# Row halves for two heads at once: maxima and scores of a transformer layer on one core of Trainium2

## The chip, the core and the metric

The kernel runs on one core of a Trainium2 chip. The core has five engines with a queue each: TensorE (PE in the profile; PEld are its weight loads), VectorE (DVE), ScalarE (ACT), GpSimd (POOL) and SyncE (SP), which here issues nearly all transfers. Operands lie in SBUF, products land in eight banks of PSUM, 512 f32 columns wide. The metric is the time of one execution in microseconds (us).

## The reference

Four sequences of 1,024 rows and 256 columns go through a residual block without softmax and then through a block with 16 query heads, 4 key/value heads of 16 channels, and 8 experts of which each row takes 2.

```
x = x + attn_linear(layernorm(x))
h = rmsnorm(layernorm(x)); q, k, v = split(h @ wqkv.T); q, k = rope(q), rope(k)
scores = einsum("bqhd,bkhd->bhqk", q, k) * 16**-0.5
scores = where(causal, scores, min)
attn = softmax(scores) @ v
x = x + attn @ wo.T; h = rmsnorm(x)
out = x + sum over the two best experts of weight * ((silu(h @ w1.T) * (h @ w3.T)) @ w2.T)
```

The change is in the line with scores and in the softmax of the line after next.

## The kernel before

**Tiling.** A head group is one key head with its four query heads (GRP); there are 16 (4 sequences, 4 key heads). The 1,024 query rows are two chunks of 512 (CH; r is 0 or 1), keys go in tiles of 128 (kt). Chunk 0 needs key tiles 0 to 3, chunk 1 all eight. On the diagonal the widths are 512, 384, 256 and 128.

**Exact products in bf16.** q and k are f32, split into three bf16 parts each (stage `split`). Six of the nine products of parts count; a head has 16 channels, so the six make one contraction of 96 rows. `split_store` writes the parts to DRAM (`parts`, 3 x 320 rows), and `stack` reads them back into a *stack*, an SBUF buffer with 96 rows of queries for four heads and 96 of keys. Keys' rows and queries' rows need another order, so the three `KPARTS` are loaded apart, with two transfers each. There are three stacks (NSTACK), so loads run ahead of use.

**Maxima** (`max`, L1871 to L1890 on TensorE, L1699 to L1708 on VectorE). For each query tile of 128 rows (jj) and head, TensorE forms all products with the keys up to the diagonal and adds a mask of -1e38 by a product of `identb` and `causal` (L1889, or L1879 for four heads at once). VectorE reduces the columns to one maximum per row (`mx`). In chunk 1 a unit is one head: 512 columns against chunk 0's keys (L1883) in one bank, w own columns (L1888) and the mask in the next, one reduce over CH + w columns. `maxT` (L1894) transposes the maxima, VectorE negates them into two bf16 parts (`mneg_parts`, L1715 and L1717), and SyncE writes these to rows 96 and 97 of the stack (L979).

**Scores** (`score`, L1901). A contraction of 98 rows now gives score minus maximum, 512 columns (or less on the diagonal) of one head per bank; up to four narrow ones share a bank. ScalarE takes the exponential into `probs` (L1254), GpSimd masks the diagonal tiles (L1115), and `pv` (L1915) forms the weighted sums of the four heads in four column groups of the array, 17 columns each, in f32.

**Order.** `plan()` walks through all steps once, before the kernel is built, with a table of assumed durations and due times, and picks for each engine the next step; all five instruction orders and the PSUM banks (RING, seven of them; the eighth holds the weighted sums) come from it. `seat` gives a step its banks. Where `keep_warm` sees TensorE idle it puts in a `warm` step (L1804, or L1801 where two neighbouring banks are free: 64-row products in either half of the array). Each engine runs its list in order. The experts' steps are due last and fill gaps from the third sequence on.

## Time and profile before

| | |
|---|---|
| median of 3 runs | 1,112.95 us (1,111.84 to 1,113.57) |
| the profiled execution | 1,115.85 us, span 1,114.1 us |
| granted TensorE clock, mean | 0.996 of full speed |
| busy: PE, DVE, ACT, POOL | 1,078.1, 737.3, 576.5, 408.4 us |
| maxima's reduces on VectorE | 352, 346.8 us |
| exponentials of the scores on ScalarE | 608, 309.0 us |

The span is the stretch from the first to the last instruction of the profiled execution; its own time is 1.75 us longer. PE's busy time counts each matmul to its end, though the next one starts earlier, so the distance of starts is what one costs. What the rows say of a wait is in the engine's idle time before a group and in the releaser that ended it.

### The profile page before, as it was taken

The numbers are of one execution on the slowest core, as the hardware profiler recorded it, in microseconds if no ns is written. First come the engines' busy times: TensorE is split into PE (matmuls) and PEld (weight loads), VectorE is DVE, ScalarE is ACT, GpSimd is POOL, SyncE is SP. The second block draws the span as 40 slices with busy tenths as digits, with TensorE's granted clock in tenths as the row PEclk, the third lists the DMA queues.
The fourth block names the chain that finished last, engine by engine and source line by source line (L and its number), as shares of the span: only waits on it lengthen the run. The fifth ranks groups of instructions, "written<-read, shape, count | busy, mean of one in ns | idle before, by whom it ended". The sixth has DMA issues, their size and how long they took to land.

```text
span 1114.1 us, 20589 instructions
## 1 busy us (share of the span) xinstructions
PE 1078.1 (97%) x7168; PEld 677.9 (61%) x7168; DVE 737.3 (66%) x1522; ACT 576.5 (52%) x1108; POOL 408.4 (37%) x476
## 2 busy tenths in 40 slices
PE   6999999999999999999999999999999999999997
PEld 5666543554544333444344454446667999999996
DVE  4697998677677977578967669624347555555552
ACT  3554477556658887756556765562332222233220
POOL 1020413616541154321244522445544753333332
PEclk9999999999999999999999999999999999999999
DMA  6324222232226466551253441124342543222221
GB/s 178 121 84 136 69 73 62 79 102 73 86 90 177 137 206 189 160 147 44 53 138 89 110 115 41 35 61 94 83 103 54 106 86 49 46 45 44 45 44 11
DMA packets 85717, 102.07 MB, mean 92 GB/s; under 512 B 17104, under 2 KB 73296, under 8 KB 85616
## 3 DMA queue, kind: packets, MB, share of 16 engines
q1 hardware_dynamic: 71312, 81.13, 25.5%
q0 software_dynamic: 14304, 19.63, 9.5%
q8 instruction: 59, 0.97, 0.4%
q14 instruction: 42, 0.34, 0.1%
HBM read 55.89 MB, written 41.01 MB: 87 GB/s over the span
## 4 chain that ended last, share of the span: by engine, by line
PE 75%; DVE 16%; issue 2%; DMA 2%; ACT 2%; SPq 1%; POOL 1%; DVEq 0%; POOLq 0%
PE psum L1970 15%; PE psum L1986 11%; PE psum L1915 9%; DVE mx L1708 8%; PE psum L1962 8%; PE psum L1901 8%; PE psum L1888 4%; PE psum L1883 4%; PE psum L1869 3%; PE psum L1922 3%; PE psum L1823 2%; PE psum L1889 1%; PE psum L1950 1%; PE psum L1845 1%; PE psum L1937 1%
## 5 line engine op out<-in xcount | busy, mean ns | idle before, releaser
L1708 DVE TENSOR_REDUCE mx<-psum 128x1 f32<-128x640 f32 (+6 forms) x352 | 346.8, 1022 | 73.5 <-PE psum L1889 68.9
L1254 ACT ACTIVATE probs_mem<-psum 128x512 f32<-128x512 f32 (+1 forms) x608 | 309.0, 586 | 142.1 <-PE psum L1901 140.5
L1115 POOL TENSOR_SCALAR_AFFINE_SELECT probs_mem<-probs_mem 128x512 f32<-128x512 f32 x128 | 82.1, 642 | 293.0 <-ACT probs_mem L1254 292.5
L1160 POOL DMA_INDIRECT out<-yout,labels x71 | 112.7, 1588 | 207.9 <-DVE yout L1774 151.8
L1901 PE MATMUL psum<-stack_mem 98*128 98x512 bf16 (+3 forms) x768 | 172.5, 327 | 4.2 <-DVE mx L1708 3.5
L1915 PE MATMUL psum<-probs_mem,v 128*17 128x512 f32 (+3 forms) x1536 | 160.4, 492 | 1.6 <-POOL probs_mem L1115 1.3
L1888 PE MATMUL psum<-stack_mem 96*128 96x256 bf16 (+3 forms) x448 | 124.8, 311 | 0.8 <-DVE mx L1708 0.6
L1901 PEld LDWEIGHTS psum<-stack_mem 98*128 98x128 bf16 x768 | 63.9, 98 | 86.3 <-DVE mx L1708 31.1
L1883 PE MATMUL psum<-stack_mem 96*128 96x512 bf16 x256 | 97.2, 385 | 5.9 <-DVE mx L1708 3.2
L1962 PE MATMUL psum<-w_mem,blockT 128*128 x200 | 96.8, 607 | 1.9 <-issue 1.8
L1889 PE MATMUL psum<-causal,identb 128*128 128x128 bf16 x448 | 96.2, 220 | 0.0
L1986 PE MATMUL psum<-w_mem,gatedT 128*128 x384 | 91.3, 381 | 0.0
L1970 PE MATMUL psum<-blockT,probs_mem 128*128 128x128 f32 x736 | 89.6, 275 | 0.0
L1970 PE MATMUL psum<-blockT,stack_mem 128*128 128x128 f32 x736 | 89.5, 275 | 0.0
L1970 PEld LDWEIGHTS psum<-blockT,probs_mem 128*128 128x128 f32 x736 | 87.6, 192 | 1.2
L1970 PEld LDWEIGHTS psum<-blockT,stack_mem 128*128 128x128 f32 x736 | 87.5, 192 | 1.2
L1282 ACT ACTIVATE gated<-psum 128x512 f32<-128x512 f32 x48 | 28.7, 598 | 108.2 <-PE psum L1962 58.3
L1986 PEld LDWEIGHTS psum<-w_mem,gatedT 128*128 128x128 f32 x384 | 70.5, 190 | 14.4 <-issue 6.4
L1145 POOL DMA_INDIRECT routed<-hrow,route_mem x64 | 64.4, 1006 | 35.8 <-issue 18.1
L1758 DVE COPY blockT<-psum 128x256 f32<-128x256 f32 x71 | 30.0, 422 | 70.6 <-PE psum L1950 70.5
L1888 PEld LDWEIGHTS psum<-stack_mem 96*128 96x128 bf16 x448 | 44.0, 98 | 32.0 <-issue 12.6
L1889 PEld LDWEIGHTS psum<-causal,identb 128*128 128x128 bf16 x448 | 43.6, 97 | 32.1 <-issue 0.6
(209 smaller groups left out, 1518.9 us busy)
## 6 DMA issues: line engine op xcount, KB each, us to landing
block<-routed SPq DMA_DIRECT2D x71, 129.0 KB, 2.1
w_mem<-in_w13T SPq DMA_DIRECT2D x16, 512.0 KB, 5.1
qk_parts<-w_mem SPq DMA_DIRECT2D x16, 384.0 KB, 2.5
stack_mem<-qk_parts SPq DMA_DIRECT2D x32, 192.0 KB, 3.2
...
```

The costliest lines, as they stand in the source:

```text
L1115: e.affine_select(pb[:, :, q0:q0 + P], pb[:, :, q0:q0 + P], [[0, GRP], [1, P]], ALU.is_ge, 0.0, base=0, channel_multiplier=-1).then_inc(se ...
L1160: e.indirect_dma_start(out_rows, bass.IndirectOffsetOnAxis(ap=labels[w % NLABEL].bitcast(I32)[:, 0:1], axis=0), youts[w % NYOUT], None, bo ...
L1254: e.activation(probs[m % 2][:, hh:hh + n, q0:CH], grid(turn[step][0][:, 0:n * (CH - q0)], n), ACT.Exp, scale=float(HD) ** -0.5).then_inc(s ...
L1708: e.tensor_reduce(to, took, AX.X, ALU.max).then_inc(sem["max"], 1)
L1883: e.matmul(bk[:, 0:CH], rows_of, s[0:STACK, 0, GRP, :], start=True, stop=True)
L1888: e.matmul(to, rows_of, s[0:STACK, r, GRP, 0:w], start=True, stop=False)
L1889: m = e.matmul(to[:, w - P:w], identb, causal, start=False, stop=True)
L1901: m = e.matmul(bk[:, i * (CH - q0):(i + 1) * (CH - q0)], s[0:STACK + NMAX, kt // TPR, GRP, kt % TPR * P:(kt % TPR + 1) * P], s[0:STACK + N ...
L1915: m = e.matmul(pv_bank[32 * hh:32 * hh + HD + 1, q0:CH], v1[:, b, kt, g, :], pb[:, hh, q0:CH], start=(kt == KEYS[r][0]), stop=(kt == KEYS[ ...
L1962: m = e.matmul(bk, blockT[w % 2][:, k], w13_s[:, k, bass.ds(offset[w] + half * FFN, FFN)], start=(k == 0), stop=(k == KD - 1))
L1970: m = e.matmul(bk[:, c * P:(c + 1) * P], slots[w % NSLOT][:, k, half * FFN + c * P:half * FFN + (c + 1) * P], blockT[w % 2][:, k], start=( ...
L1986: m = e.matmul(bk[:, 0:D], rowsT[:, k * P:(k + 1) * P], w2_mem[:, bass.ds(offset[w] + k * D, D)], start=(k == 0), stop=(k == KF - 1))
```

## The change

- **Halves.** The array is used as two halves of 64 rows (SIDES). Heads 0 and 1 of a group lie on rows 0 to 63, heads 2 and 3 on rows 64 to 127 (PER_SIDE). Each matmul of `max` and `score` has 64 rows or fewer and comes twice, once for each half, into neighbouring banks.
- **Maxima** are formed from four of the six products of parts, the 64 rows of the first stack (FIRST). The mask is added in pieces that fit 64 rows: 64 columns with `causal`'s triangle, then 128 columns. In chunk 1 the products against chunk 0's keys are units of their own, with their own column of `mx`, and a `tensor_tensor` joins both sets. Reduces take both halves at once.
- **Scores** are two passes per half: 64 rows of the first stack, then 34 of the second (two products and the two rows of negated maxima). A step covers both halves in two banks; ScalarE's exponential takes up to 1,024 columns.
- **Stacks.** Two in place of one: three buffers of the first (NFIRST), two of the second (NSECOND). Outside, in DRAM, `q_image` and `k_image` hold the rows in the stacks' order, parts repeated as needed (96 rows per head in place of 48), so each split unit is stored by three transfers (SPLIT_STORES) and a stack is loaded by 3 (first) or 4 (second, mostly for both chunks at once). The negated maxima go by four transfers.
- **Order.** `plan()` gets the new units, two banks for each score, and a preference to stay in one division of the array (STAY; `division`: row halves, column groups, or neither). `warm` has only its f32 form.

```diff
-KPARTS = (3, 2, 1)
-STACK = sum(KPARTS) * HD
+SIDES = 2
+PER_SIDE = GRP // SIDES
+SIDE = P // SIDES
+FIRST, SECOND = 4 * HD, 2 * HD
 NMAX = 2
+SPLIT_STORES = 3
...
-NSTACK = 3
+NFIRST, NSECOND = 3, 2
...
+STACK_LOADS = (SIDES + 1, 2 * SIDES)
...
-    if r:
-        return [(jj, hh, 1, CH, (jj + 1) * P) for jj in range(TPR) for hh in range(GRP)]
-    units = []
+    units = [(False, jj, h0, 1, CH) for jj in range(TPR) for h0 in range(PER_SIDE)] if r else []
     for jj in range(TPR):
-        w = (jj + 1) * P
-        nh = GRP if jj < 2 else 2
-        units += [(jj, h0, nh, w if jj < 2 else CH, w) for h0 in range(0, GRP, nh)]
+        n = PER_SIDE if jj < 2 else 1
+        units += [(True, jj, h0, n, (jj + 1) * P) for h0 in range(0, PER_SIDE, n)]
     return units
-def max_banks(r, u):
-    return 1 if not r and max_units(r)[u][0] == 0 else 2
 def heads_in(r, kt):
-    n = min(GRP, CH // (CH - max(kt * P - r * CH, 0)))
-    return n, range(0, GRP, n)
+    n = min(PER_SIDE, CH // (CH - max(kt * P - r * CH, 0)))
+    return n, range(0, PER_SIDE, n)
...
+        own, jj, h0, n, w = max_units(r)[u]
+        joined = 0.25 * (r > 0 and u == len(max_units(r)) - 1)
+        return ("PE", n * (w + 3 * SIDE * own) / 2400 + 0.02), ("DVE", 0.07 + SIDES * n * w / 960 + joined)
...
         if stage == "score":
             n = heads_in(r, kt)[0]
-            return ("PE", n * w / 2400 + 0.01), ("ACT", 0.06 + n * w / 1200)
+            return ("PE", 2 * n * w / 2400 + 0.02), ("ACT", 0.06 + SIDES * n * w / 1200)
         last = kt == KEYS[r][-1]
-        return (("PE", 0.23 + w / 600), ("ACT", 0.49)) if last else (("PE", 0.23 + w / 600),)
+        return (("PE", 0.13 + w / 600), ("ACT", 0.49)) if last else (("PE", 0.13 + w / 600),)
...
+    def division(step):
+        return {"score": 1, "max": 1, "pv": 2}.get(step[0], 0)
...
-            return [("max", *at, len(max_units(at[2])) - 1)] + [("maxT", *chunk_at(m))] * (m >= 0)
+            freed = [s for n in group_back(b, at[1], NSECOND) for s in last_scores(*n)]
+            return [("max", *at, len(max_units(at[2])) - 1)] + [("maxT", *chunk_at(m))] * (m >= 0) + freed
...
-            return [("maxT", *at[:3])] + [pvs[m]] * (m >= 0)
+            return [("maxT", *at[:3])] + [("stack", b, at[1], c, 1) for c in (range(at[2] + 1) if not at[1] else [QR - 1])] + [pvs[m]] * (m >= 0)
...
-        n = max_banks(*step[3:]) if step[0] == "max" else KD if step[:2] == ("gram", 0) else 1
+        n = SIDES if step[0] in ("max", "score") else KD if step[:2] == ("gram", 0) else 1
...
+            later = STAY * (engine == "PE" and division(step) != divided)
+            key = (0, due + later, start) if start <= free + 0.05 else (1, start, due)
...
-            end += COLD * (start > clock[engine] + COLD)
+            end += COLD * (start > clock[engine] + COLD or division(step) != divided)
...
-                    r0, n = ((NH * HD, 2 * HK), (0, P), (P, P))[u]
-                    q.wait_ge(*slot("split_store", 4, m - 4))
...
+                    q.wait_ge(*slot("split_store", 4, m - 4, SPLIT_STORES))
...
-                    e.dma_start(parts[b][:, c, r0:r0 + n, :].rearrange("s r t -> r s t"), splits[m % 2][0:n]).then_inc(sem[f"split_store{m % 4}"], 16)
+                    for part, at_rows in enumerate(found):
...
+                        e.dma_start(to, splits[m % 2][0:n, part].unsqueeze(1).broadcast_to([n, len(at_rows), CH])).then_inc(sem[f"split_store{m % 4}"], 16)
                 elif stage == "stack":
...
-                    e.dma_start(s[to:to + nk * HD, c, GRP, :], parts[b][0:nk, c, NH * HD + g:QK:NKV, :].rearrange("s i t -> i s t")).then_inc(landing, 16)
-                    e.dma_start(s[to:to + nk * HD, c, 0:GRP, :].rearrange("p h t -> p (h t)"),
-                                q_rows(b, qp, c)[g].unsqueeze(1).broadcast_to([HD, nk, GRP * CH])).then_inc(landing, 16)
+                    b, g, c, of_second = at
+                    n = b * NKV + g
+                    landed(q, "split_store", 4, 3 * (QR * b + c + 1), SPLIT_STORES)
+                    if not of_second:
+                        s, landing = first[n % NFIRST], sem[f"first{n % NFIRST}_{c}"]
+                        if n >= NFIRST:
+                            first_read(q, *HEAD_GROUPS[n - NFIRST])
+                        e.dma_start(s[:, c, PER_SIDE, :], key_rows(b, g)[c, SECOND:].unsqueeze(0).broadcast_to([SIDES, FIRST, CH])).then_inc(landing, 16)
+                        for side in range(SIDES):
+                            e.dma_start(s[side * SIDE:(side + 1) * SIDE, c, 0:PER_SIDE, :].rearrange("p h t -> p (h t)"), side_rows(b, g, side)[c, SECOND:]
+                                        ).then_inc(landing, 16)
+                    else:
+                        s, landing = second[n % NSECOND], sem[f"second{n % NSECOND}_{c}"]
+                        if n >= NSECOND:
+                            second_read(q, *HEAD_GROUPS[n - NSECOND])
+                        cs = slice(0 if g else c, c + 1)
+                        for side in range(SIDES):
+                            to = s[side * SIDE:side * SIDE + SECOND, cs]
+                            e.dma_start(to[:, :, PER_SIDE, :], key_rows(b, g)[cs, 0:SECOND].rearrange("c r t -> r c t")).then_inc(landing, 16)
+                            e.dma_start(to[:, :, 0:PER_SIDE, :].rearrange("p c h t -> p c (h t)"), side_rows(b, g, side)[cs, 0:SECOND].rearrange("c r t -> r c t")).then_inc(landing, 16)
                 elif stage == "maxT":
                     b, g, r = at
...
+                    if n >= NSECOND:
+                        second_read(q, *HEAD_GROUPS[n - NSECOND])
+                    for side in range(SIDES):
+                        for c in range(NMAX):
+                            row, of = side * SIDE + SECOND + c, side * PER_SIDE * TPR
+                            e.dma_start(second[n % NSECOND][row:row + 1, r, 0:PER_SIDE, :].rearrange("p h t -> p (h t)"), mneg_parts[of:of + PER_SIDE * TPR, c, :]
+                                        ).then_inc(sem[f"max_load{m % 2}"], 16)
...
+                    scored = grid(turn[step][0], SIDES)[:, :, 0:n * (CH - q0)].rearrange("p s (h q) -> p s h q", h=n)
                     q.wait_ge("score_mm", nth[step])
                     q.wait_ge("pv_mm", m - 1)
-                    e.activation(probs[m % 2][:, hh:hh + n, q0:CH], grid(turn[step][0][:, 0:n * (CH - q0)], n), ACT.Exp, scale=float(HD) ** -0.5).then_inc(sem["exp"], 1)
+                    e.activation(probs[m % 2].rearrange("p (s h) q -> p s h q", s=SIDES)[:, :, hh:hh + n, q0:CH], scored, ACT.Exp, scale=float(HD) ** -0.5).then_inc(sem["exp"], 1)
...
+                    own, jj, h0, n, w = max_units(r)[u]
+                    to = mx[:, r if own else 2].rearrange("p (s h j) -> p s h j", s=SIDES, h=PER_SIDE)[:, :, h0:h0 + n, jj]
+                    took = grid(turn[step][0], SIDES)[:, :, 0:n * w].rearrange("p s (h k) -> p s h k", h=n)
                     q.wait_ge("max_mm", nth[step])
                     q.wait_ge("maxT_mm", chunk(b, g, r) - 1)
                     e.tensor_reduce(to, took, AX.X, ALU.max).then_inc(sem["max"], 1)
+                    if r and u == len(max_units(r)) - 1:
+                        q.wait_ge("max", nth[step])
+                        e.tensor_tensor(mx[:, 1], mx[:, 1], mx[:, 2], ALU.max).then_inc(sem["join"], 1)
...
-                    jj, h0, nh, pitch, w = max_units(r)[u]
-                    s = stack[(b * NKV + g) % NSTACK]
-                    buffer_loaded(q, b, g, r)
-                    q.wait_ge("const", 4)
-                    if w == P and not r:
-                        e.matmul(grid(bk, GRP), identb, causal.unsqueeze(1).broadcast_to([P, GRP, P]), start=True, stop=False)
-                    for c in range(nh):
-                        rows_of = s[0:STACK, r, h0 + c, jj * P:(jj + 1) * P]
-                        if r:
-                            e.matmul(bk[:, 0:CH], rows_of, s[0:STACK, 0, GRP, :], start=True, stop=True)
-                        to = bk[:, CH:CH + w] if r else bk[:, c * pitch:c * pitch + w]
-                        if w == P and not r:
-                            m = e.matmul(to, rows_of, s[0:STACK, r, GRP, 0:w], start=False, stop=c == nh - 1)
-                        else:
-                            e.matmul(to, rows_of, s[0:STACK, r, GRP, 0:w], start=True, stop=False)
-                            m = e.matmul(to[:, w - P:w], identb, causal, start=False, stop=True)
+                    own, jj, h0, n, w = max_units(r)[u]
+                    s = first[(b * NKV + g) % NFIRST]
+                    first_loaded(q, b, g, r)
+                    q.wait_ge("const", 6)
+                    for c in range(n):
+                        halves = [(slice(i * SIDE, (i + 1) * SIDE), bk[:, i * CH + c * w:i * CH + (c + 1) * w]) for i in range(SIDES)]
+                        for half, to in halves:
+                            m = e.matmul(to, s[half, r, h0 + c, jj * P:(jj + 1) * P], s[half, r if own else 0, PER_SIDE, 0:w], start=True, stop=not own)
+                        if own:
+                            for half, to in halves:
+                                e.matmul(to[:, w - SIDE:w], diagonal[half, 0:P], causal[half, 0:SIDE], start=False, stop=False)
+                            for half, to in halves:
+                                m = e.matmul(to[:, w - P:w], diagonal[half, SIDE:], causal[half], start=False, stop=True)
                     m.then_inc(sem["max_mm"], 1)
                 elif stage == "maxT":
                     b, g, r = at
-                    q.wait_ge("max", nth["max", b, g, r, len(max_units(r)) - 1])
+                    if r:
+                        q.wait_ge("join", b * NKV + g + 1)
+                    else:
+                        q.wait_ge("max", nth["max", b, g, r, len(max_units(r)) - 1])
                     e.transpose(bk[0:16, 0:P], mx[:, r], ident).then_inc(sem["maxT_mm"], 1)
                 elif stage == "score":
                     b, g, r, kt, hh = at
-                    q0, n, s = max(kt * P - r * CH, 0), heads_in(r, kt)[0], stack[(b * NKV + g) % NSTACK]
-                    q.wait_ge(*slot("max_load", 2, chunk(b, g, r), NMAX))
-                    q.wait_ge("set", 6)
+                    q0, n, m_of = max(kt * P - r * CH, 0), heads_in(r, kt)[0], b * NKV + g
+                    w, tile = CH - q0, slice(kt % TPR * P, (kt % TPR + 1) * P)
+                    q.wait_ge(*slot("max_load", 2, chunk(b, g, r), NMAX * SIDES))
+                    q.wait_ge("set", 7)
+                    first_loaded(q, b, g, r)
+                    second_loaded(q, b, g, r)
                     for i in range(n):
-                        m = e.matmul(bk[:, i * (CH - q0):(i + 1) * (CH - q0)], s[0:STACK + NMAX, kt // TPR, GRP, kt % TPR * P:(kt % TPR + 1) * P],
-                                     s[0:STACK + NMAX, r, hh + i, q0:CH], start=True, stop=True)
+                        for s, rows_in in ((first[m_of % NFIRST], FIRST), (second[m_of % NSECOND], SECOND + NMAX)):
+                            for side in range(SIDES):
+                                half = slice(side * SIDE, side * SIDE + rows_in)
+                                m = e.matmul(bk[:, side * CH + i * w:side * CH + (i + 1) * w], s[half, kt // TPR, PER_SIDE, tile], s[half, r, hh + i, q0:CH],
+                                             start=rows_in == FIRST, stop=rows_in != FIRST)
```

**TensorE, batch 1, second head group, chunk 1.** In the first fence each head's maxima are three multiplies (L1883 against chunk 0's keys, L1888 own keys, L1889 mask), and L1901 are scores, L1915 weighted sums, L1922 the output product.

```order
L1883 MATMUL psum<-stack_mem 128x512
L1888 MATMUL psum<-stack_mem 128x256
L1889 MATMUL psum<-causal,identb 128x128
L1901 MATMUL psum<-stack_mem 128x512
L1883 MATMUL psum<-stack_mem 128x512
L1888 MATMUL psum<-stack_mem 128x256
L1889 MATMUL psum<-causal,identb 128x128
L1915 MATMUL psum<-probs_mem,v 17x512 x4
L1883 MATMUL psum<-stack_mem 128x512
L1888 MATMUL psum<-stack_mem 128x256
L1889 MATMUL psum<-causal,identb 128x128
L1901 MATMUL psum<-stack_mem 128x384 x4
```

The same group and chunk after, at two places of the changed order (L1952 products, L1956 and L1958 mask pieces, L1980 scores, L1994 weighted sums, L1875 a warm-up): the products against chunk 0's keys first,

```order
L1952 MATMUL psum<-stack_mem 128x512 x4
L1980 MATMUL psum<-stack_mem 128x512 x4
L1994 MATMUL psum<-probs_mem,v 17x128 x4
L1980 MATMUL psum<-stack_mem 128x512 x4
L1952 MATMUL psum<-stack_mem 128x512 x4
L1875 MATMUL psum<-ident 128x128
L1980 MATMUL psum<-stack_mem 128x512 x8
L1994 MATMUL psum<-probs_mem,v 17x512 x4
```

and those against its own keys behind them.

```order
L1952 MATMUL psum<-stack_mem 128x256 x2
L1956 MATMUL psum<-causal,diagonal 128x64 x2
L1958 MATMUL psum<-causal,diagonal 128x128 x2
L1980 MATMUL psum<-stack_mem 128x256 x8
L1994 MATMUL psum<-probs_mem,v 17x512 x4
L1952 MATMUL psum<-stack_mem 128x384 x2
L1956 MATMUL psum<-causal,diagonal 128x64 x2
L1958 MATMUL psum<-causal,diagonal 128x128 x2
```

Three multiplies per head became six per pair of heads on own keys and one per head against chunk 0's; scores are twice as many multiplies, each of half the rows. Between scores, sums and f32 work the array's division now changes each time.

**SyncE at the start: stores and first loads of sequence 0, chunk 0.** Before (L962 stores of split parts, L970 keys and L971 queries of a stack):

```order
L962 DMA qk_parts<-w_mem 64x3x512
L962 DMA qk_parts<-w_mem 128x3x512 x2
L970 DMA stack_mem<-qk_parts 48x1x512
L971 DMA stack_mem<-qk_parts 48x1x2048
L970 DMA stack_mem<-qk_parts 32x1x512
L971 DMA stack_mem<-qk_parts 32x1x2048
L970 DMA stack_mem<-qk_parts 16x512
L971 DMA stack_mem<-qk_parts 16x2048
```

After (L1015 stores of the images, L1024 and L1026 the first stack, L1035 and L1036 the second):

```order
L1015 DMA q_image<-w_mem 128x3x512
L1015 DMA q_image<-w_mem 128x2x512
L1015 DMA q_image<-w_mem 128x512
L1024 DMA stack_mem<-k_image 128x1x512
L1026 DMA stack_mem<-q_image 64x1024 x2
L1035 DMA stack_mem<-k_image 32x512
L1036 DMA stack_mem<-q_image 32x1024
L1035 DMA stack_mem<-k_image 32x512
L1036 DMA stack_mem<-q_image 32x1024
```

Three stores became nine (the last three stand here), and the six loads ahead of the first maximum became three, with four more behind them for the scores.

## Rows read from the trace of the kernel before

**Rows 1.** The page, part 1: busy time, share of the span, instructions of each engine.
```profile
PE 1078.1 (97%) x7168; PEld 677.9 (61%) x7168; DVE 737.3 (66%) x1522; ACT 576.5 (52%) x1108; POOL 408.4 (37%) x476
```
**Rows 2.** Groups of TensorE by form, then its timeline (start us, us, engine line).
```profile
L1901 PE MATMUL psum<-stack_mem 98*128 98x512 bf16 x384 | 110.0, 380 | 3.2 <-DVE mx L1708 2.8 <-ACT probs_mem L1254 0.2
...
309.68 1.04 PE L1901 MATMUL psum<-stack_mem 98*128 98x512 bf16 x4
...
310.81 0.22 PE L1888 MATMUL psum<-stack_mem 96*128 96x128 bf16 x1
310.87 0.22 PE L1889 MATMUL psum<-causal,identb 128*128 128x128 bf16 x1
```
**Rows 3.** The page, part 4: the chain that ended last, by engine.
```profile
PE 75%; DVE 16%; issue 2%; DMA 2%; ACT 2%; SPq 1%; POOL 1%; DVEq 0%; POOLq 0%
```
**Rows 4.** Who waited for whom: us in total, times, longest.
```profile
ACT probs_mem L1254 <- PE psum L1901: 140.5, 141, 4.6
...
DVE mx L1708 <- PE psum L1889: 68.9, 77, 4.0
...
PEld psum L1901 <- DVE mx L1708: 31.1, 51, 2.3
...
PEld psum L1883 <- DVE mx L1708: 21.3, 41, 1.0
```
**Rows 5.** Warm-ups in row halves: their group by form, then TensorE's timeline at two places.
```profile
L1801 PE MATMUL psum<-causal,identb 64*128 64x256 bf16 x56 | 4.4, 272 | 0.1
...
36.02 0.49 PE L1801 MATMUL psum<-causal,identb 64*128 64x256 bf16 x6
...
305.83 0.72 PE L1804 MATMUL psum<-ident 128*128 128x128 f32 x5
306.49 0.39 PE L1801 MATMUL psum<-causal,identb 64*128 64x256 bf16 x4
```
**Rows 6.** TensorE's timeline from a score through column groups to a maximum.
```profile
299.98 0.33 PE L1901 MATMUL psum<-stack_mem 98*128 98x384 bf16 x1
300.24 1.05 PE L1915 MATMUL psum<-probs_mem,v 128*17 128x512 f32 x8
301.22 0.28 PE L1888 MATMUL psum<-stack_mem 96*128 96x256 bf16 x1
```
**Rows 7.** Weighted sums of 128 columns: by form, and one step in the timeline.
```profile
L1915 PE MATMUL psum<-probs_mem,v 128*17 128x128 f32 x256 | 13.2, 278 | 0.1
...
745.21 0.41 PE L1915 MATMUL psum<-probs_mem,v 128*17 128x128 f32 x8
```
**Rows 8.** The maxima's reduces on VectorE, by form.
```profile
L1708 DVE TENSOR_REDUCE mx<-psum 128x1 f32<-128x1024 f32 x64 | 75.9, 1218 | 16.9 <-PE psum L1889 16.7
...
L1708 DVE TENSOR_REDUCE mx<-psum 128x1 f32<-128x640 f32 x64 | 50.1, 810 | 13.8 <-PE psum L1889 13.5
```
**Rows 9.** Exponentials of 512 columns on ScalarE, by form.
```profile
L1254 ACT ACTIVATE probs_mem<-psum 128x512 f32<-128x512 f32 x480 | 255.6, 608 | 117.5 <-PE psum L1901 116.1 <-issue 0.5
```
**Rows 10.** SyncE's and TensorE's timeline: stack loads, negated maxima, a chunk's first score.
```profile
63.28 0.62 SPq L970 DMA_DIRECT2D stack_mem<-qk_parts  x1
...
371.46 1.16 SPq L979 DMA_DIRECT2D stack_mem<-mneg_parts  x2
...
380.74 0.39 PE L1901 MATMUL psum<-stack_mem 98*128 98x512 bf16 x1
...
90.84 1.19 PE L1901 MATMUL psum<-stack_mem 98*128 98x512 bf16 x5
```
**Rows 11.** Windows of 50 us: PE, PEld, DVE, ACT, POOL busy (count), clock, DMA share, GB/s.
```profile
100.00:150.00 50.00, 49.12 (x324) 26.83 (x324) 47.33 (x88) 21.32 (x40) 14.40 (x15) 1.00 0.23 72
...
250.00:300.00 50.00, 49.24 (x331) 23.92 (x330) 33.98 (x49) 31.98 (x64) 26.91 (x27) 1.00 0.27 79
...
350.00:400.00 50.00, 47.84 (x361) 18.85 (x363) 46.77 (x93) 40.35 (x74) 11.82 (x16) 1.00 0.59 170
...
500.00:550.00 50.00, 47.39 (x333) 21.91 (x332) 44.08 (x97) 30.29 (x61) 10.88 (x15) 0.98 0.22 60
```

158 lines of the change are left out of this document (86 added, 72 removed), and 1 row of the table WORK_OF.

## The prediction

> **What bounds the kernel now.** Page first: TensorE is busy 97% of the span, VectorE 66% [rows 1]. A busy TensorE isn't a full one: 512-column multiplies that last 380 ns start 0.22 us apart ((1.04 - 0.38) / 3), 128-column ones 0.06 us apart [rows 2]. I multiplied these distances by the order's counts: a column costs 0.42 ns in bf16, four times that in f32 and twice in an f32 transpose. The maxima then take 150 us, scores 123, weighted sums 123 (four heads together in column groups), experts 389, all else 170: some 955 us of 1,114, and the rest is switches, short starts and waits. The chain of waits agrees: 75% TensorE, 16% VectorE [rows 3]. The table of waits says what the rest is. TensorE's loads wait for the maxima's reduces to give banks back (31.1 and 21.3 us), and the reduces wait for their products (68.9 us); ScalarE waits 140.5 us for scores [rows 4]. So TensorE is the bound and VectorE the next one; ScalarE and GpSimd have room.
>
> **1. Columns saved in the maxima.** Now, per head group: chunk 0 streams 7,168 columns (5,120 of products, 2,048 of mask), chunk 1 15,360 (8,192 against chunk 0's keys, 5,120, 2,048). After, each matmul has 64 rows and a half of the array. If two halves run together, a pair costs one: chunk 0 has 2 x (1,280 + 4 x 192) = 4,096, chunk 1 8 x 512 + 4,096 = 8,192. Saved: 10,240 columns x 16 groups = 163,840, or 320 x 0.217 us = **-69 us**. That halves do run together is in the trace: three pairs of 64-row, 256-column warm-ups took 0.49 us where one multiply takes 0.27, so 0.11 us per pair, the time of one [rows 5].
>
> **2. Scores.** 98 rows become 64 + 34 on either half: four multiplies for two heads where there were two. Two passes on two halves stream what two full passes did: **0**, if rows 5 hold for accumulating pairs too.
>
> **3. Switches of the array's division.** After a 384-column score at 299.98 the sums in column groups start at 300.24, where 300.14 was due; after their two passes of 0.43 us the next maximum starts at 301.22, where 301.11 was due [rows 6]. Full to row halves is the same: a 128-column warm-up started at 306.28 (305.83 + 0.72 - 0.27), the halves at 306.49, 0.10 late [rows 5]. So 0.10 us each way. Before, scores and maxima shared the full array with all f32 work; after, they have a division of their own. Counted over the whole order without warm-ups, switches go from 370 to 595: 225 x 0.097 = **+22 us**.
>
> **4. Small multiplies.** The mask becomes a 64- and a 128-column pair per product pair, so six loads and six multiplies stand where w = 128 streams only 0.133 us. The densest rate shown is four loads and four multiplies in a pass of 0.107 us, 0.027 us each [rows 7]: 6 x 0.027 = 0.16, +0.03 us in 64 places, 2 us. If a 64-column pair needed 2 x 0.027 wherever it stands, 256 pairs cost +7 us. With some ns of offset in each pair I take **+3 us**. TensorE's sum: -69 + 22 + 3 = **-44 us**.
>
> **5. VectorE.** A reduce costs 1.06 ns per column ((1,218 - 810) / 384) and about 0.13 us fixed [rows 8]. Columns stay the same; 22 reduces per group become 20 and a join of 128x16. Before 22.5 us, after 22.2 + 0.2: **0**. It is what I expect to be late next.
>
> **6. ScalarE.** 608 exponentials become 320 of up to 1,024 columns. At 608 ns for 512 columns [rows 9], of which 0.43 us stream, that saves at most 0.18 x 288 = 52 us of an engine that waits for TensorE. On the path **0**; without the cover it would help.
>
> **7. SyncE, and what stands behind it.** Its transfers go from 657 to 753, about 0.58 us each [rows 10]. Negated maxima go in four issues in place of two, +1.2 us. Behind them stand stack loads and the packs; who waits is the scores. At the tightest place past the start they land with room: issued at 371.46, first score at 380.74 [rows 10], over 8 us later. Hidden. At the start nothing hides them: the last unit's store of queries is three issues, not one (+1.2), and twice the bytes must land; against that, three loads and not six (0.62 us each) stand ahead of the first maximum (-1.9); then come four issues of negated maxima (+1.2) and the second stack. Bounds 0 and +6, taken **+2 us**. A score now holds two banks of seven; no row prices that, and it is in the range.
>
> **How much arrives.** Of ten stretches of 50 us from 100 to 600, VectorE is busy 95, 94 and 88% in three; the rest lie at 63 to 84%, as 250:300 [rows 11]. In the three a faster TensorE only waits longer for banks, unless the order shifts work. In the other seven, and after 600, where expert blocks fill what attention leaves, it can arrive. I take two thirds: -29 us, with the start -27, and the 1 us that the reduces wait less is **-28 us**. The profiled execution took 1,115.85 us (span 1,114.1), so 1,087.9 by its own time. The median of the runs is 2.9 us under it: **1,085 us**.
>
> A rule of the skill speaks against the change. The Trainium skill, TensorEngine Tiling (Array Packing), section PSUM Bottleneck, says that tiling speeds TensorE but not the emptying of PSUM, which may then bind. By the three full stretches the trace agrees; by the other seven it doesn't yet.
>
> **Rivals.**
> - *VectorE takes over.* For it: the 52 us of loads that wait for reduces [rows 4]; and the whole order is a compromise between the two engines, so that a stretch at 75% may already be held by VectorE's bursts. Then only a third of 44 arrives: -15, and with the start 1,100 us. Against it: 68.9 us in which the reduces themselves wait for products. Chance 0.18.
> - *All of it arrives*, since products come sooner and the reduces' own waits shrink: -44 and up to 4 more, with the start 1,068 us. 0.13.
> - *Rate of small multiplies, mild.* If in row halves a load with its multiply takes the 0.055 us at which full 128-column ones follow each other [rows 2], the products on own keys cost 6 x 0.055 in place of (w + 192) x 0.42 ns, 30 us in all, and 128-column scores 7 us more: TensorE -10, with the start 1,105 us. 0.05.
> - *Slower.* The same mechanism from 0.060 us on: there it costs the 47 us that columns and switches leave. At 0.062 us it is +52 us, so TensorE +5 and 1,120 us. Halves that don't overlap when they accumulate are its end: maxima 164 us in place of 82, scores 246 in place of 123, about 1,270 us. The 0.027 us of rows 7 and the warm-ups of rows 5 speak against it; but rows 7 load 17 columns, not 128, and rows 5 stream 256, so neither shows a 128-column load in 0.027. 0.10.
> - *The change does what it says and nothing arrives*: 1,111 to 1,115. 0.04.
>
> The Trainium skill, TensorE: Matmul & The Clock Gate, section "Wait — 56ns, not 53.3ns?", gives about 62 ns of sequencer time per multiply with hardware decode off, the slow rival's case; the four multiplies of a pass in rows 7 speak against that here.
>
> **How the numbers follow.** Forecast (1,072 to 1,097) 0.50, VectorE 0.18, all 0.13, mild rate 0.05, slower 0.10, nothing 0.04. The likeliest is 1,085. From 1,066 to 1,108 lie the forecast, VectorE, mild rate and half of "all": about 0.8. The three runs lie within 0.16%, so 0.2% is about what can be told. Faster 0.86; within 0.2% 0.04; slower 0.10.
>
> **What would show it.** Steps 1 and 2: in the timeline the two halves' multiplies start together, a pair of 512 columns every 0.22 us; right if the maxima's multiplies per group fit in some 5 us. Step 3: 0.1 us at each change between scores, sums and f32 work. Step 4: a chain of load, 64 and 128 columns of 0.08 us behind its product; 0.17 would be the mild rival. Step 5: reduces still some 345 us in all, TensorE's waits for them longer than 52 us, their waits for products under 69. Step 7: first score at about 93 us, not 91. The prediction is wrong if the halves start one behind the other, or if VectorE stands above 90% through most of 100 to 600.

## The result, and the profile after

The changed kernel takes 1,123.15 us (median of 6 runs, 1,122.41 to 1,127.17); the kernel before, on the same chip, 1,113.26. The ratio is **1.0091, 95% interval 1.0068 to 1.0114**: 10 us slower, where I forecast 28 us faster. The profiled execution took 1,122.6 us (span 1,120.9).

The page of the changed kernel, parts 1, 4 and 5:

```profile
PE 1059.8 (95%) x8560; PEld 651.0 (58%) x8560; DVE 747.9 (67%) x1510; ACT 560.9 (50%) x820; POOL 411.1 (37%) x477
...
PE 66%; DVE 17%; SPq 5%; DMA 4%; ACT 3%; issue 3%; POOL 1%; DVEq 0%; POOLq 0%; ACTq 0%
...
L1782 DVE TENSOR_REDUCE mx<-psum 128x2 f32<-128x1024 f32 (+2 forms) x320 | 344.3, 1111 | 67.7 <-PE psum L1958 42.7
L1324 ACT ACTIVATE probs_mem<-psum 128x1024 f32<-128x1024 f32 (+1 forms) x320 | 289.5, 936 | 141.6 <-PE psum L1980 140.2
```

TensorE is 2 points less busy than in [rows 1] over a longer span. In the chain its share falls from 75 to 66% [rows 3]; VectorE stays, and what has grown is SyncE's queue with the transfers, from 3 to 9%. The work itself went as predicted, which TensorE's timeline shows (start us, us, engine line, tiles, count):

```profile
299.96 0.41 PE L1994 MATMUL psum<-probs_mem,v 128*17 128x128 f32 x8
300.30 0.23 PE L1952 MATMUL psum<-stack_mem 64*128 64x128 bf16 x2
300.37 0.19 PE L1956 MATMUL psum<-causal,diagonal 64*128 64x64 bf16 x2
300.40 0.22 PE L1958 MATMUL psum<-causal,diagonal 64*128 64x128 bf16 x2
300.45 0.22 PE L1952 MATMUL psum<-stack_mem 64*128 64x128 bf16 x2
...
300.60 1.03 PE L1980 MATMUL psum<-stack_mem 64*128 64x512 bf16 x8
301.64 0.28 PE L1952 MATMUL psum<-stack_mem 64*128 64x256 bf16 x2
...
301.83 0.29 PE L1952 MATMUL psum<-stack_mem 64*128 64x256 bf16 x2
...
301.97 0.24 PE L1958 MATMUL psum<-causal,diagonal 64*128 64x128 bf16 x2
302.14 1.05 PE L1994 MATMUL psum<-probs_mem,v 128*17 128x512 f32 x8
303.12 0.34 PE L1952 MATMUL psum<-stack_mem 64*128 64x384 bf16 x2
...
313.03 0.39 PE L1952 MATMUL psum<-stack_mem 64*128 64x512 bf16 x2
```

Two multiplies of 512 columns, one on each half, take 0.39 us together (313.03), what one takes alone (0.38). The eight score multiplies from 300.60 are four pairs, each second pair adding to what the one before it left; with 0.38 us for the last pair they start (1.03 - 0.38) / 3 = 0.22 us apart. Behind a 128-column product (300.30) its masks start 0.07 and 0.10 us later, and the next product 0.15. A product's last mask starts at 301.97 and would let a successor of the same division start at 302.03 (an estimate: 0.06 us for 128 columns, as in [rows 2]); the weighted sums start at 302.14, so the change of division costs 0.1 us.

To see where the time went I added up, over the whole trace, the distances from each multiply's start to the next, and split each into what its columns stream, up to 0.1 us at a change of division, up to 5 ns of issue, and a rest, called stalls below. All of it is worked out from the records of the one profiled execution of each kernel, and good to 1 or 2 us; "maxima" and "scores" are the streamed columns at full clock (us):

| | maxima | scores | changes | warm-ups | issue | stalls | other | all |
|---|---|---|---|---|---|---|---|---|
| before | 150.2 | 122.9 | 37.2 | 9.3 | 20.5 | 70.8 | 687.6 | 1,098.5 |
| after | 84.5 | 125.5 | 61.6 | 19.0 | 16.7 | 111.2 | 687.5 | 1,105.9 |

So 66 us were saved, and the changes of division cost 24, as predicted. **Forty us of stalls** took the rest, more than half of what there was before on top of it, and the warm-ups that the planner puts into such gaps doubled (+9.7). Who waits for whom (us in total, times, longest):

```profile
ACT probs_mem L1324 <- PE psum L1980: 140.2, 126, 10.3
...
DVE mx L1782 <- PE psum L1958: 42.7, 49, 3.6
...
PEld psum L1980 <- DVE mx L1782: 42.4, 69, 1.8
...
PEld psum L1952 <- DVE mx L1782: 34.2, 55, 2.4
...
PEld psum L1952 <- ACT probs_mem L1324: 26.9, 43, 1.9
...
DVE mx L1782 <- PE psum L1952: 23.0, 24, 2.7
```

TensorE's loads now wait 76.6 us for the reduces, where it was 52.4 [rows 4]. The reduces wait for two kinds of product now, 42.7 and 23.0 us. A load's wait is not yet a stall, since loads run ahead of the multiplies. Sorted by what released the late multiply or its load (worked out from the records), the stalls behind the maxima's steps on VectorE grow from 16 to 26 us, **those behind ScalarE's exponentials from 6 to 17**, those behind GpSimd from 3 to 6; 36 before and 44 after show no wait that released them. So it is not VectorE alone that TensorE runs into.

The windows that answer to [rows 11], and two more, show no engine behind TensorE that is full (the number before the last two is the granted clock):

```profile
100.00:150.00 50.00, 44.53 (x362) 25.74 (x360) 41.90 (x83) 16.20 (x23) 13.14 (x13) 0.93 0.38 124
250.00:300.00 50.00, 45.37 (x407) 18.89 (x407) 37.63 (x49) 32.29 (x47) 30.64 (x31) 1.00 0.47 128
350.00:400.00 50.00, 45.92 (x452) 21.80 (x452) 36.25 (x80) 35.29 (x48) 5.94 (x10) 1.00 0.49 149
400.00:450.00 50.00, 42.77 (x486) 15.58 (x485) 39.48 (x55) 35.55 (x40) 19.09 (x22) 0.97 0.59 174
450.00:500.00 50.00, 44.20 (x427) 18.28 (x427) 31.84 (x44) 32.58 (x54) 21.87 (x32) 0.97 0.65 183
500.00:550.00 50.00, 47.54 (x416) 21.49 (x418) 43.02 (x99) 28.21 (x42) 7.70 (x13) 1.00 0.28 69
```

VectorE is even less busy than before in three of the four windows of [rows 11].

The granted clock is part of the loss, and no step of the prediction prices it. In the profiled execution TensorE ran at the lower level (1.2 of 2.4 GHz) for 6.8 us in two stretches before the change and for 13.6 us in three after it, the last 4 us of either span aside. Those three, from 122.0, 415.6 and 480.4 us, begin during a stall of 4.1 us or within 2 us of the end of one of 3.0 us. So a stall can be paid twice, once in waiting and once in the clock behind it; the stalls of the table hold what the lower level cost, some 3 us before and 5 to 6 after. In the 59 executions of the kernel before, each compared with the others on its chip, 0.001 less of mean clock goes with 1.1 us more. The changed kernel's six have 0.991 on average where those have 0.995, so by this **some 5 of its 10 us came with the clock** (an estimate; no run sets the clock apart).

By 80 us from 320 on, the stalls were 8.4 and 7.0 before and are 14.5 and 19.9 after. There the chain runs through SyncE (start us, us, what):

```profile
414.67 0.29 DVE mneg_parts L1792
...
414.99 0.29 DVE mneg_parts L1794
...
415.34 0.70 SPq L1047
...
417.47 0.63 SPq L1047
...
418.15 0.44 SPq L1035
...
421.17 0.56 SPq L1060
...
439.02 0.58 SPq L1091
...
439.65 8.98 DMA w_mem<-in_w13T
```

SyncE has waited for VectorE's negated maxima (called the bounds from here on; L1047 are their transfers) and then issues for 24 us with hardly a pause what had piled up behind them: loads of stacks (L1035), packs of finished heads (L1060), the next bounds, a load of weights (L1091).

### The profile page after: what moved, and what is told of

Read it like the earlier page. It is cut to its first block, busy times and chain, and to the rows that moved or that the text cites. A ratio compares the mean times of both kernels' runs of the same rounds, so it can differ in the third digit from the quotient of the medians.

```text
span 1120.9 us, 23078 instructions
## 1 busy us (share of the span) xinstructions
PE 1059.8 (95%) x8560; PEld 651.0 (58%) x8560; DVE 747.9 (67%) x1510; ACT 560.9 (50%) x820; POOL 411.1 (37%) x477
## 4 chain that ended last, share of the span: by engine, by line
PE 66%; DVE 17%; SPq 5%; DMA 4%; ACT 3%; issue 3%; POOL 1%; DVEq 0%; POOLq 0%; ACTq 0%
PE psum L2049 15%; PE psum L2065 11%; DVE mx L1782 8%; PE psum L2041 7%; PE psum L1994 7%; PE psum L1980 7%; PE psum L1952 3%; PE psum L2001 3%; PE psum L1940 2%; ACT probs_mem L1324 2%; PE psum L1894 2%; PE psum L2029 1%; PE psum L2016 1%; SPq L1047 1%; SPq L1026 1%
## 5 line engine op out<-in xcount | busy, mean ns | idle before, releaser
L1782 DVE TENSOR_REDUCE mx<-psum 128x2 f32<-128x1024 f32 (+2 forms) x320 | 344.3, 1111 | 67.7 <-PE psum L1958 42.7
L1324 ACT ACTIVATE probs_mem<-psum 128x1024 f32<-128x1024 f32 (+1 forms) x320 | 289.5, 936 | 141.6 <-PE psum L1980 140.2
L1184 POOL TENSOR_SCALAR_AFFINE_SELECT probs_mem<-probs_mem 128x512 f32<-128x512 f32 x128 | 85.9, 672 | 291.7 <-ACT probs_mem L1324 291.5
L1980 PE MATMUL psum<-stack_mem 64*128 64x512 bf16 (+7 forms) x1536 | 168.0, 326 | 15.2 <-DVE mx L1782 7.4
L1994 PE MATMUL psum<-probs_mem,v 128*17 128x512 f32 (+3 forms) x1536 | 160.3, 495 | 2.6 <-POOL probs_mem L1184 1.2
L1952 PE MATMUL psum<-stack_mem 64*128 64x512 bf16 (+3 forms) x768 | 114.7, 330 | 15.1 <-DVE mx L1782 5.6
L1980 PEld LDWEIGHTS psum<-stack_mem 64*128 64x128 bf16 (+1 forms) x1536 | 55.3, 94 | 106.2 <-DVE mx L1782 42.4
L1952 PEld LDWEIGHTS psum<-stack_mem 64*128 64x128 bf16 x768 | 36.3, 94 | 108.1 <-issue 35.0
L1851 DVE TENSOR_SCALAR yout<-psum,labels 128x256 f32<-128x256 f32 x71 | 34.3, 483 | 39.2 <-PE psum L2065 35.5
L1994 PEld LDWEIGHTS psum<-probs_mem,v 128*17 128x17 f32 x1536 | 26.8, 96 | 56.3 <-issue 31.4
L1841 DVE SCALAR_TENSOR_TENSOR gated<-gated,psum 128x512 f32<-128x512 f32 x48 | 33.0, 687 | 35.4 <-ACT gated L1352 35.2
```

Source lines behind the costliest of these rows:

```text
L1184: e.affine_select(pb[:, :, q0:q0 + P], pb[:, :, q0:q0 + P], [[0, GRP], [1, P]], ALU.is_ge, 0.0, base=0, channel_multiplier=-1).then_inc(se ...
L1324: e.activation(probs[m % 2].rearrange("p (s h) q -> p s h q", s=SIDES)[:, :, hh:hh + n, q0:CH], scored, ACT.Exp, scale=float(HD) ** -0.5). ...
L1782: e.tensor_reduce(to, took, AX.X, ALU.max).then_inc(sem["max"], 1)
L1851: e.tensor_scalar(youts[w % NYOUT], turn[step][0][:, 0:D], labels[w % NLABEL][:, 1:2], None, ALU.mult).then_inc(sem["y"], 1)
L1952: m = e.matmul(to, s[half, r, h0 + c, jj * P:(jj + 1) * P], s[half, r if own else 0, PER_SIDE, 0:w], start=True, stop=not own)
L1980: m = e.matmul(bk[:, side * CH + i * w:side * CH + (i + 1) * w], s[half, kt // TPR, PER_SIDE, tile], s[half, r, hh + i, q0:CH], start=rows ...
```

## The experiments

Eighteen kernels; those named b_ start from the kernel before, those named a_ from the changed one. "Us" is the ratio less one times the time of before; "to after" compares with the changed kernel's +10.1, whose own interval is +-2.5 us. "Stalls" as in the table above, from one execution each, the lower clock's cost included.

| kernel | ratio to before (95%) | us | stalls |
|---|---|---|---|
| b_pe | 0.9896 (0.9867 to 0.9926) | -11.6 | 110.4 |
| b_dve | 0.9922 (0.9903 to 0.9940) | -8.7 | 61.7 |
| b_pe_dve | 0.9716 (0.9685 to 0.9747) | -31.7 | 89.7 |
| a_dve | 0.9968 (0.9948 to 0.9989) | -3.6, to after -13.7 | 103.1 |
| a_both | 0.9921 (0.9891 to 0.9951) | -8.8, to after -18.9 | 95.4 |
| b_sp | 1.0085 (1.0053 to 1.0117) | +9.5 | 84.4 |
| b_mneg | 1.0082 (1.0054 to 1.0109) | +9.1 | 79.6 |
| b_pair | 1.0029 (1.0016 to 1.0042) | +3.2 | 72.9 |
| b_sp_pe | 1.0053 (1.0028 to 1.0079) | +5.9 | 113.0 |
| b_pair_pe | 0.9950 (0.9927 to 0.9974) | -5.6 | 103.8 |
| b_three | 1.0161 (1.0135 to 1.0186) | +17.9 | 117.6 |
| b_div | 1.0130 (1.0097 to 1.0163) | +14.5 | 69.2 |
| b_other | 1.0043 (1.0023 to 1.0063) | +4.8 | 79.8 |
| a_ahead | 1.0162 (1.0137 to 1.0187) | +18.1, to after +8 | 114.7 |
| a_stay0 | 1.0297 (1.0262 to 1.0332) | +33.1, to after +23 | 113.4 |
| a_few | 1.0085 (1.0061 to 1.0108) | +9.5, to after -0.7 | 115.4 |
| a_one | 1.0057 (1.0035 to 1.0080) | +6.4, to after -3.8 | 112.1 |
| b_one | 0.9950 (0.9930 to 0.9970) | -5.6 | 69.4 |

### What is TensorE time in the maxima worth? (b_pe, b_pe_dve, b_dve)

```diff
-e.matmul(bk[:, 0:CH], rows_of, s[0:STACK, 0, GRP, :], ...)
+e.matmul(bk[:, 0:64], rows_of, s[0:STACK, 0, GRP, 0:64], ...)       # b_pe, b_pe_dve
-took = took[:, 0:CH + w].unsqueeze(1) if r else ...
+took = took[:, 0:CH + w:2].unsqueeze(1) if r else ...               # b_dve, b_pe_dve
```

> The kernel before with its order unchanged; each of the 256 products of a second chunk's maxima with the first chunk's keys moves 64 columns in place of 512 (448 x 256 / 2,400 = 47.8 us less on TensorE), while VectorE's reduces read as much as before, so part of what they reduce is left over from earlier products. It asks what TensorE time taken out of the maxima is worth in the kernel before. If two thirds of it arrives, as I predicted, the time falls by about 32 us to 1,081. If VectorE's reduces, ScalarE's exponentials and the order set attention's pace, less than a third arrives: -15 us or less, and TensorE's stalls grow by the rest.

> The kernel before in its order with two cuts together: the 256 first-chunk products of the maxima move 64 columns in place of 512, as in b_pe (-47.8 us on TensorE), and each reduce of a second chunk reads every other column (VectorE about 110 us less). b_pe alone gave -11.6 us with 110 us of stalls. If VectorE's queue is what the saved TensorE time ran into, it comes through here: -35 us or more against before. If order, transfers and ScalarE hold the rest, no more than -20 us.

> The kernel before in its order with VectorE's reduces of the second chunks reading every other column (about 110 us less on VectorE) and TensorE as before. With b_pe (-11.6) and b_pe_dve (-31.7) it closes the square: if VectorE were a wall of its own before the change, this alone gives -15 us or more; if it only catches TensorE's time once that is saved, less than 8 us.

Of the 47.8 us taken from TensorE, **11.6 arrive, a quarter**. The stalls grow by 39.6, to 110.4, what the changed kernel has. Sorted as above, 14 of these 40 us stand behind reduces, 6 behind exponentials, and 9 in stretches at the lower clock. In the trace of b_pe, the waits with the reduces, and the chain from 158 us:

```profile
DVE mx L1708 <- PE psum L1889: 60.2, 64, 3.6
...
PEld psum L1901 <- DVE mx L1708: 35.8, 57, 2.8
...
PEld psum L1883 <- DVE mx L1708: 29.4, 56, 1.6
```

```profile
158.01 0.69 DVE w_mem L1652
...
160.83 1.55 DVE mx L1708 x2
...
164.65 0.68 DVE w_mem L1672
...
166.79 3.42 DVE mx L1708 x4
...
170.40 2.86 DVE mx L1708 x3
...
174.38 2.00 DVE mx L1708 x2
```

L1652 to L1674 are the next sequence's norms and rotations. VectorE works for 18 us with hardly a gap here: reduces queue behind them, and the products wait for the banks that the reduces give back. With the second chunks' reduces halved too, 31.7 us arrive; now the reduces wait for products, and TensorE's loads wait 37.5 us for them in place of 65.2. In b_pe_dve:

```profile
DVE mx L1708 <- PE psum L1889: 112.0, 107, 4.5
...
PEld psum L1901 <- DVE mx L1708: 26.1, 42, 0.9
...
PEld psum L1883 <- DVE mx L1708: 11.4, 17, 1.0
```

The 108 us less on VectorE (its reduces take 238.9 us, for 346.8) give 8.7 alone, the TensorE cut 11.6 alone, both 31.7: 11 us come only when both are had. So the two engines are bound to each other. b_pe fell where its second theory said. b_pe_dve, at 31.7, is short of the 35 us that would have made VectorE the whole of it: on top of the shorter reduces the cut gives 23.0 of 47.8 us, half in place of a quarter. Shown is that **VectorE's reduces hold back a quarter of the cut**; half of it doesn't arrive even so, and there the stalls behind exponentials are 19 us, those behind reduces 6.

### Relief inside the changed kernel (a_dve, a_both)

```diff
-took = grid(turn[step][0], SIDES)[...].rearrange("p s (h k) -> p s h k", h=n)
+took = grid(turn[step][0], SIDES)[...].rearrange("p s (h k) -> p s h k", h=n)[:, :, :, 0:w // 2]
-e.activation(probs[...][:, :, hh:hh + n, q0:CH], scored, ACT.Exp, ...)            # a_both also; upto: half of the CH - q0 columns
+e.activation(probs[...][:, :, hh:hh + n, q0:q0 + upto], scored[:, :, :, 0:upto], ACT.Exp, ...)
```

> The changed kernel with its order unchanged, and VectorE's reduces of the maxima reading only the first half of each tile's keys (so the bounds come from half the keys): VectorE has about 160 us less to do in the maxima and nothing else changes. If VectorE's pace is what swallowed the TensorE time that the halves saved, most of the 40 us of added stalls goes and the time falls by 25 to 40 us against the changed kernel (to 1,085 to 1,098). If the pace is set by transfers, by banks or by the order, it falls by less than 8 us.

> The changed kernel in its order, with the reduces over half of each tile's keys as in a_dve and, after the first two key tiles, the exponentials over half of each tile's queries (the other half of the probabilities keeps older values): ScalarE about 140 us less. a_dve alone gave about -13 us. If ScalarE and the banks its exponentials hold are the second wall, another -15 us or more (1,100 or less); if the order and its latencies are, less than 6 us more.

VectorE has 149 us of reduces less (195.4 for 344.3), and 13.7 us come of it; ScalarE's relief adds 5. The 13.7 lie between what the two theories of a_dve said; the 5 are under 6, where a_both's second theory (order and latencies) put them. 95 us of stalls remain with both engines relieved: from 320 to 480 us there are 40.6, against 15.4 before, in the stretch of SyncE's unbroken issues; some 8 of them are the lower clock's. VectorE is a wall here, not the only one.

### The transfers (b_sp, b_mneg, a_few)

```diff
 e.dma_start(parts[b][:, c, r0:r0 + n, :]..., splits[m % 2][0:n])...
+for i in range(2):                                                   # b_sp only
+    e.dma_start(more_parts[m, i, :, 0:n]..., splits[m % 2][0:n])...
 for c in range(NMAX):
     e.dma_start(s[STACK + c:STACK + c + 1, r, 0:GRP, :]..., mneg_parts[:, c, :])...
+    e.dma_start(more_rows[m, c], mneg_parts[:, c, :])...             # b_sp, b_mneg
```

> The kernel before with its order unchanged and the changed kernel's added transfers alone: each of the 24 stores of the split columns is followed by two more of the same size to memory that nothing reads, and each chunk's bounds go out with two more transfers (64 more in all), all of which are waited for like the first ones. SyncE has 112 issues more, about 65 us. If the transfers are what gave the saving back, this costs 20 to 40 us (1,133 to 1,153). If the queue has room for them, less than 5 us.

> The kernel before in its order with only the 64 added transfers of the bounds (two more for each chunk, waited for like the first two); the split columns are stored once as before. If the bounds' transfers, which stand between VectorE's bounds and a chunk's first score, make b_sp's cost, 6 us or more slower than before; if the 48 added stores make it, within 3 us.

a_few changes the changed kernel's store: `for part, at_rows in enumerate(found[:1] if b else found)`, and `side_rows` and `key_rows` read image 0.

> The changed kernel in its order with fewer stores: the last three sequences store their split columns once in place of three times (36 issues and half of those bytes less), and their stacks are loaded from the first sequence's image at the same times (so they hold the wrong rows). If the added transfers hold the changed kernel back through SyncE's queue, it is 5 to 12 us faster than the changed kernel (1,110 to 1,118), most of it between 160 and 480 us. If only their order or latency matter, within 3 us.

My "hidden" for SyncE was wrong: the transfers cost 9.5 us, and the 64 of the bounds 9.1 of them; stores cost nothing that the intervals can tell, neither added here (0.4 us) nor taken away in a_few (0.7). That the added transfers land later isn't what costs: VectorE's step that writes the bounds waits 7.7 us in all, as before (7.6), and hardly a score waits for a landing. What fits is the bounds' place: they wait for VectorE at the head of SyncE's queue, and the stack loads, packs and reciprocals of other steps stand behind. The chain of b_mneg:

```profile
435.85 0.29 DVE mneg_parts L1720
436.20 0.53 SPq L981
...
439.26 0.57 SPq L972
...
441.88 0.58 SPq L992
...
450.41 0.58 SPq L983
...
451.03 3.84 DMA recips<-sums
...
457.38 8.75 DMA block<-routed
```

From bounds to reciprocals 15 us go by in issues, and 7 of the 9 us of added stalls lie between 400 and 480 us. Some 4 of these 9 us are the cost of the lower clock, in two stretches from 405 and 467 us. No run takes the bounds' transfers out of the in-order queue, so its part stays argued from the chain.

### Two-bank scores, and whether the parts add (b_pair, b_pair_pe, b_sp_pe, b_three)

```diff
-n = min(GRP, CH // (CH - max(kt * P - r * CH, 0)))
+n = min(GRP, 2 * (CH // (CH - max(kt * P - r * CH, 0))))             # heads of a score
-n = max_banks(...) if step[0] == "max" else ...
+n = 2 if step[0] == "score" else max_banks(...) if step[0] == "max" else ...
```

> The kernel before with its scores formed in units of two banks (two heads of 512 columns, or four of 256 or fewer, and one exponential over both banks) as in the changed kernel, still on the whole array and with its stacks and transfers as before; the planner makes its order anew. ScalarE saves the fixed cost of about 190 exponentials. If the coarser units and the two banks a score holds cause the added stalls, it costs 15 to 40 us (1,128 to 1,153); if they don't, it is within 8 us of before.

> The kernel before with three things together: scores in two-bank units (b_pair), the changed kernel's added transfers (b_sp), and the first-chunk products of the maxima cut from 512 to 64 columns in the last three sequences (192 x 448 / 2,400 = 35.8 us less on TensorE, nearly the 42.5 us that the change takes from TensorE in sum; the reduces read as much as before). If the parts simply add, it is -8.7 + 9.5 + 3.3 = 4 us slower than before, 1,117 to 1,124, and the change is explained by its parts. If it is faster than before by 3 us or more, something in the changed kernel that none of the three has (the divisions, the second stack, its order) makes the loss.

> The kernel before in its order with the changed kernel's added transfers (b_sp, +9.5 us alone) and the first-chunk products of the maxima cut to 64 columns in the last three sequences (35.8 us less on TensorE). If the two simply add, about before +1 us. If the transfers are a wall behind which no saved TensorE time arrives, it equals b_sp: +9 us or more against before, and the two-bank units are not needed to explain b_three (+18).

> The kernel before with two-bank scores (b_pair, +3.3 us alone) and the same cut of 35.8 us on TensorE, and no added transfers. If the parts add, about before -5 us. If coarse units are what keeps saved TensorE time from arriving, it stays at +3 us or more; then b_three's +18 comes from this pair and not from the transfers.

The two-bank units, with 288 exponentials fewer and an order of their own, cost 3.2 us alone, at a higher mean clock (0.998 for 0.995); with the cut they add as expected (-5.6). The transfers and the cut don't: +5.9 where +0.8 was the sum, so hardly 4 of 36 us arrive, between the two theories. Part of that is the clock: b_sp_pe averages 0.985 for 0.995, some 11 us by the rate found above. All three give +17.9 for 4 expected. So **a loss of this kind appears without one added change of division and without the second stack**: coarser units, more transfers and cheaper maxima are enough for it, and make more together than apart. That the changed kernel's own loss is made so isn't shown by it. b_pair's order is a new one, so some of the 14 us that don't add may be the order's; how many, is open.

### Changes of the division (b_div, a_stay0)

```diff
+n64 = 4 * HD if jj < 2 else STACK
-e.matmul(bk[:, 0:CH], rows_of, s[0:STACK, 0, GRP, :], ...)
+e.matmul(bk[:, 0:CH], rows_of[0:n64], s[0:n64, 0, GRP, :], ...)
```

> The kernel before in its order with 128 of the first-chunk products of the maxima on 64 rows in place of 96 (they leave out the two smallest of six terms), as many columns as before: about 250 more changes of the array's division, the number that the change adds, at 0.09 to 0.10 us each 23 to 25 us on TensorE. If TensorE time arrives in full when it is added, about +24 us. If it is partly swallowed by waits that are there anyway, as saved time is, +6 to +15 us.

a_stay0 sets STAY to 0 and drops the change from the test that adds COLD.

> The changed kernel with a planner that neither puts off a change of the array's division (3 tiles before) nor charges 0.1 us for it: 720 changes in the planned order in place of 637, 157 warm-ups in place of 89. By the switch rate of 0.097 us the changes alone cost 8 us and the warm-ups 15 us where nothing covers them: slower than the changed kernel by 8 to 20 us if the changes lie on the path. If the putting off had cost more in stalls than it saved in changes, it is faster by 5 us or more.

b_div has 617 changes for 384 and 23.2 us more in them; 14.5 +- 3.7 arrive in the medians, 20.8 in the profiled execution, whose clock was the lowest of its four (0.987 for 0.994 to 0.996). a_stay0 has 14.5 us more of warm-ups and 8.1 of changes, and all 23 us arrive, in another order (see below for what that alone can move). **In these runs TensorE time that is added arrives by more than half; time that is taken away, by a quarter.** The cut was twice as large as what b_div adds and sat at other products; a cut of the same size at the same place was not run.

### How much is chance of the order? (b_other, a_ahead)

```diff
-AHEAD = {"DVE": 1.7, "ACT": 1.9}
+AHEAD = {"DVE": 1.7, "ACT": 2.0}        # b_other, from before
+AHEAD = {"DVE": 2.2, "ACT": 2.4}        # a_ahead, from after
```

> The kernel before with one number of the planner moved (the backlog it lets ScalarE have, 1.9 to 2.0 us) and nothing else: another order of the same work. It measures how much of a difference between two planned orders is chance. If order alone moves the time by several us either way, it lies 3 us or more from before; if the plan is robust, within 2 us.

> The changed kernel with the planner allowing VectorE and ScalarE more backlog (2.2 and 2.4 us in place of 1.7 and 1.9), so that TensorE runs further ahead of them: another order of the same work (662 changes of division in place of 637). If the added stalls are short waits for banks and reduces that a longer lead covers, 8 us or more faster than the changed kernel; if it is chance of the order, within 6 us either way.

The same work in another order cost 4.8 us in before and, with 2 us more of changes and longer leads, 8 in after. A longer lead covers none of the stalls (114.7 for 111.2). So, as far as two other orders can tell, any comparison of two planned orders here, the change itself included, carries some 5 to 8 us that no step explains.

### One number for each bound (b_one, a_one)

```diff
-NMAX = 2
+NMAX = 1
-e.scalar_tensor_tensor(mneg_parts[:, 1], bk[0:16, 0:P], -1.0, mneg_parts[:, 0], ...)
```

> The kernel before with each query's bound as one bf16 number in place of two (NMAX = 1; the same number is subtracted from all scores of a query, so the softmax is what it was): 32 transfers fewer, 32 of VectorE's smallest steps (0.28 us each, 9 us) fewer, the same order. b_mneg's 64 added transfers cost 9.1 us; if the cost is linear in their number, this gives -4.5 us, and up to -2 us more for VectorE. If SyncE's queue only hurts above what the kernel before puts on it, within 2 us of before.

> The changed kernel with one number for each bound in the same way: 64 transfers fewer (the number that the change added) and 32 small VectorE steps fewer, in its own order. If the bounds' transfers are what they were in b_mneg, it is about 9 us faster than the changed kernel, at the time of before (ratio 0.998 to 1.003). If, as with the stores, fewer transfers give nothing in the changed kernel, its ratio stays at 1.007 or more, and its loss lies in its order and its chain of units.

In the changed kernel, taking out as many transfers of bounds as it had added gives 3.8 us, little more than the intervals can tell (1.0035 to 1.0080 against 1.0068 to 1.0114), and its stalls stay. So the bounds' transfers are at most a part of its loss. In before the same edit, which also takes 9 us of small steps from VectorE, gives 5.6 us: b_one, at 0.9950, **beats both kernels**. Its page, part 4:

```profile
PE 79%; DVE 14%; issue 2%; ACT 2%; DMA 1%; POOL 1%; another core or an unknown queue 0%; SPq 0%; POOLq 0%; DVEq 0%; ACTq 0%
```

SyncE's queue has left the chain, and TensorE has gone from 75 to 79%.

## Why the prediction was wrong

**Its own signs.** Neither sign that was to show the prediction wrong came: the halves start together, and VectorE stands between 64 and 86% in every window of 50 us from 100 to 600. The two engines' waits moved as forecast (76.6 us, over 52; 65.7 with both kinds of product, under 69). Only the first score missed its sign, at 87.8 us for 93. So the signs watched the sizes of the steps and not the step that failed.

**What bounds the kernel now.** Right that TensorE is first and VectorE next; wrong in treating the second as far off. b_pe and b_pe_dve show it right behind, and ScalarE's exponentials not far behind it.

**1 to 4, TensorE's sum.** Right. Forecast -69, 0, +22, +3; in the trace -65.7, +2.6 and +24.4, with the small multiplies inside the first two and 3.8 less of issue: -42.5 for -44. Outside the sum stand 9.7 us more of warm-ups, which it didn't have. Halves overlap, the slow rivals of small multiplies are out: a chain of load, 64 and 128 columns takes 0.08 us behind what its product streams, as I wrote (301.64 to 301.83 for a product of 256 columns, which streams 0.11).

**5. VectorE.** Right in size: its reduces take 344 us. What I named as "late next" was late already.

**6. ScalarE.** Fewer exponentials saved 19 us of its work, inside the bound of 52. Wrong was the 0 on the path: TensorE's stalls behind exponentials grow from 6 to 17 us, and a_both's relief gives 5. A score that holds two banks, which I had left to the range, is one cause that fits; b_pair prices it, fewer exponentials and a new order together, at 3.2 us.

**7. SyncE.** Wrong. I asked whether the bounds land before their score, and they do. I didn't ask who else stands behind them in the queue. By b_mneg +9.1, by a_one 3.8, for the nothing that I gave them past the start. My +2 was for the start and wrong too: the first score came at 87.8 us, earlier than before (90.8).

**How much arrives** is the step that failed, and it decides the sign. I netted savings against costs (-44) and let two thirds of the net arrive, -29, since VectorE stood under 85% in seven windows of ten. Of the net nothing arrived. The runs gave each its own share: of time saved in the maxima 11.6 / 47.8 = 0.24 (b_pe), of time added by changes 14.5 / 23.2 = 0.62 (b_div). With these, -65.7 x 0.24 + 24.4 x 0.62 + 9.1 + 3.2 = +12 us, where +10.1 was measured. That the sum comes out is partly luck: the 9.1 holds some 4 us of clock and the 3.2 an order of its own, the warm-ups are left out, b_three shows that such parts don't add, and a new order alone moves 5 to 8 us. What is shown is that savings of this size mostly turn into stalls, a quarter of the cut by VectorE's reduces, while added time arrives by more than half. A part of either is the granted clock, which the prediction left at nothing: some 5 us between the two kernels, and some 6 of the 36 us that b_pe lost (0.990 on average for 0.995). How the remaining stalls split between the order, the coarse units and SyncE's queue stays open.

The window's average misled me. In 250:300 VectorE was busy 68% [rows 11], and I read that as room. But its work comes in runs like the 18 us at 158 us, and the seven banks let TensorE be only a few units ahead. The Trainium skill, TensorEngine Tiling (Array Packing), section PSUM Bottleneck, says that packing speeds the array and not the emptying of PSUM. By b_dve and b_pe_dve the runs agree in part (the cut gives 23.0 us with the reduces shortened, 11.6 without, of 47.8); I had let the seven windows speak against it. My rival "VectorE takes over" named that mechanism and gave 1,100 us; it missed the sign, because it too let the costs shrink with the savings.
